# Gated experts: how many products run in three half-width passes, and which engine makes the weight parts

## What is computed

```python
# L0: 8 experts of width 176, two chosen of 8; shared width 352
w = jnp.zeros((n, E), x.dtype).at[jnp.arange(n)[:, None], idx].add(probs)
h = jax.nn.silu(jnp.einsum('tc,ech->eth', xf, W1)) * jnp.einsum('tc,ech->eth', xf, W2)
y = jnp.einsum('eth,ehc,te->tc', h, W3, w)
hs = jax.nn.silu(xf @ Ws1) * (xf @ Ws2)
y = y + (hs @ Ws3).reshape(b, t, c)
# L1: 16 experts of width 64, four chosen of 16 in two of four groups; shared width 128
h = jax.nn.silu(g) * u
yo = jnp.einsum('tei,ehi->teh', h, down_w)
routed = jnp.einsum('te,teh->th', combine, yo)
return (routed + shared).reshape(orig_shape)
```

## Time and profile before

| | us |
|---|---|
| median of three runs | 3198.48 |
| lowest and highest | 3195.55, 3201.10 |
| the profiled execution, whole | 3196.91 |
| its span, first to last instruction | 3195.1 |
| first stage, from the start of its first PE instruction to the end of its last add on DVE | 428.40 to 574.89 |
| second stage | 632.71 to 777.44 |
| third stage | 1322.74 to 1430.86 |
| fourth stage | 1472.89 to 1570.70 |

### The profile page before, as it was taken

One profiled execution on the slowest core, in us unless ns is written; L12 is line 12 of the kernel. 1 busy time (PEld: TensorE's weight loads), 2 busy tenths in 40 slices (PEclk: granted clock), 3 DMA queues, 4 the chain that ended last, 5 costly groups with the idle time before them and its releaser, 6 DMA issues. The chain is left out here.

```text
span 3195.1 us, 58999 instructions
## 1 busy us (share of the span) xinstructions
PE 2902.7 (91%) x22885; PEld 1670.8 (52%) x22885; DVE 2175.3 (68%) x4839; ACT 1643.5 (51%) x3325; POOL 1127.0 (35%) x536
## 2 busy tenths in 40 slices
PE   7898899998999999998968897888889899998998
PEld 3333344443899999543435454444453344574547
DVE  6777645556677777667588887877861559926991
ACT  3555453433333333436467766676753557725761
POOL 1111130002100000100088787877840209912980
PEclk8999999999555555799979999999999899999999
DMA  5344323022000000030532222222302001250224
GB/s 158 91 109 99 90 91 108 3 91 84 4 4 4 4 4 4 2 109 4 187 112 95 83 90 80 87 82 83 90 27 100 4 1 80 93 198 4 95 107 177
DMA packets 113495, 234.37 MB, mean 73 GB/s; under 512 B 13760, under 2 KB 50752, under 8 KB 104768
## 3 DMA queue, kind: packets, MB, share of 16 engines
q1 hardware_dynamic: 113216, 230.59, 22.5%
HBM read 185.71 MB, written 44.83 MB: 72 GB/s over the span
## 5 line engine op out<-in xcount | busy, mean ns | idle before, releaser
L2680 DVE TENSOR_TENSOR_SCAN s_hh<-psum,s_dbu 128x512 f32<-128x512 f32 x384 | 447.6, 1208 | 71.1 <-ACT psum L2292 70.2
L1404 PE MATMUL psum<-h_ring,h_parts 128*128 128x4 f16 x12264 | 477.9, 168 | 0.6 <-DVE h_ring L1547 0.5
L2550 POOL TENSOR_TENSOR s_dbu<-s_du,s_bb 128x1024 f32<-128x1024 f32 x191 | 446.4, 2359 | 67.1 <-DVE s_hh L2680 57.1
L1404 PEld LDWEIGHTS psum<-h_ring,h_parts 128*128 128x128 f16 x12264 | 429.7, 106 | 48.6 <-DVE h_ring L1547 0.9
L1466 ACT ACTIVATE h_now<-psum 128x16 f32<-128x16 f32 x1024 | 187.9, 184 | 324.4 <-PE psum L1404 318.2
L2292 ACT ACTIVATE psum<-s_delta,s_decay 128x512 f32<-128x512 f32 x384 | 256.6, 686 | 109.9 <-DVE s_hh L2680 107.8
L2184 PEld LDWEIGHTS psum<-w_c,s_term 128*128 128x128 f32 x1536 | 197.7, 149 | 136.3 <-issue 115.8
L1547 DVE TENSOR_SCALAR h_ring<-h_now 128x16 f16<-128x16 f32 x1024 | 178.8, 175 | 117.9 <-ACT h_now L1466 77.0
L990 POOL MEMSET r_weights<- 128x512 f32 x4 | 2.1, 524 | 720.4 <-POOLq L1356 510.9
L2184 PE MATMUL psum<-w_c,s_term 128*128 128x128 f32 x1536 | 229.7, 286 | 9.6 <-ACT s_y L2370 8.5
L1549 DVE SCALAR_TENSOR_TENSOR h_ring<-h_now,h_ring 128x16 f16<-128x16 f32 x1024 | 179.5, 175 | 35.2
(11 more groups left out here) (586 smaller groups left out, 6224.1 us busy)
## 6 DMA issues: line engine op xcount, KB each, us to landing
s_bb<-s_wide SPq DMA_DIRECT2D x192, 256.0 KB, 3.4
x_spill<-x_flip SPq DMA_DIRECT2D x28, 1024.0 KB, 3.9
f_share<-f_wide SPq DMA_DIRECT2D x208, 128.0 KB, 3.0
s_cc<-s_wide SPq DMA_DIRECT2D x60, 256.0 KB, 3.4
a_ks<-a_spread SPq DMA_DIRECT2D x96, 128.0 KB, 3.3
a_qs<-a_spread SPq DMA_DIRECT2D x96, 128.0 KB, 4.0
x_spare<-x_spill SPq DMA_DIRECT2D x4, 2048.0 KB, 7.6
x_raw<-x_spill SPq DMA_DIRECT2D x4, 2048.0 KB, 7.7
```

The costliest lines, as they stand in the source:

```text
L1404: mm = nc.tensor.matmul(here[:, cols], parts[:, part, GROUP * grp + p, :], ring[:, (i - 1) % RING, grp, cut, cols], start=False, stop=True ...
L2550: nc.gpsimd.tensor_tensor(dbu[:, s % D_RING], du[:, t % 2], both(bb[:, s % B_RING, :]), ALU.mult).then_inc(dbu_ready, 1)
L2680: nc.vector.tensor_tensor_scan(hh[:, s % 4, half, :], DECAYS[i % 3], dbu[:, s % D_RING, half, :], 0.0, ALU.mult, ALU.add).then_inc(scan_do ...
```

## The change

1. In the second, third and fourth stage the three passes begin with the first chunk (`CUT_FROM` 0). DVE cuts the first chunk's inputs itself, between the norm's first and second chunk (`cut_first_inputs`).
2. From the second chunk on, in all four stages, the down products listed in `twofold` are made in three passes too: the shared tiles and every second routed one, 8 of 14 and 5 of 9 in a chunk. ACT makes the high part of the hidden tile (`keep_hi`) and POOL the rest (`keep_lo`, an f32 and an f16 input in SBUF, f16 out), in a ring of six; weights' down parts are cut as well (`MATRICES` 3). Scales are fitted to that, and the add into the residual takes one.
3. In the third stage DVE makes the weights' parts: `make_cuts(0)` and `(1)` between the norm's chunks, `(2)` behind the router. The search for the largest weight is passed over PE within the norm (`behind`). In the first stage ACT and POOL make them as before, with the third matrix added.
4. `LAG` becomes 15 and 19 in the first and second stage, 27 in the third and fourth; `TURN_AT` 18 instead of 17 in the latter two; weighings from the second chunk on stand four iterations ahead of their down product instead of two (`SOON`).

```diff
...
-LAG, AHEAD, LOGITS_AT, SQUASH_AT, EXP_AT, TURN_AT, KEEP_AT = 15, 2, 1, 1, 5, 9, 9
+AHEAD, LOGITS_AT, SQUASH_AT, TURN_AT, KEEP_AT = 2, 1, 1, 9, 9
 TURN_MOST_AT, TOP_AT, SPREAD_MOST_AT, SCALE_AT, CUT_AT = 3, 1, 4, 2, (5, 6, 9)
-WEIGHTS_EARLY = False
-BESIDE = {2: (1,), 4: (2,), 5: (3, 4), 9: (5,)}
+LAGS, EXPS_AT, WEIGHTS_EARLY = (15, 19), (5, 6), False
+BESIDES = ({2: (1,), 4: (2,), 5: (3, 4), 9: (5,)}, {1: (1,), 2: (2,), 3: (3, 4), 5: (5,), 8: (6,)})
...
-LAG, AHEAD, LOGITS_AT, SQUASH_AT, EXP_AT, TURN_AT, KEEP_AT = 24, 2, 1, 1, None, 17, 17
-TURN_MOST_AT, TOP_AT, SPREAD_MOST_AT, SCALE_AT, CUT_AT = 2, 0, 3, 1, (3, 4, 6)
-WEIGHTS_EARLY = True
-BESIDE = {n: (k + 1,) for k, n in enumerate((3, 6, 8, 9, 10, 12, 13, 14, 15, 17, 18, 19, 20, 21, 22))}
+AHEAD, LOGITS_AT, SQUASH_AT, TURN_AT, KEEP_AT = 2, 1, 1, 18, 18
+LAGS, EXPS_AT, WEIGHTS_EARLY = (27, 27), (None, None), True
+BESIDES = 2 * ({n: (k + 1,) for k, n in enumerate((3, 6, 8, 9, 10, 12, 13, 14, 15, 17, 18, 19, 20, 21, 22))},)
...
+again = int(router.pack in g.cuts_made)
+g.cuts_made.add(router.pack)
+experts, LAG, BESIDE, EXP_AT = router.experts, router.LAGS[again], router.BESIDES[again], router.EXPS_AT[again]
+cuts_first, cuts_beside = not again and router.WEIGHTS_EARLY, not again and not router.WEIGHTS_EARLY
...
-CUT_FROM, SOON, PARTS_RING = EACH, 4, 6
+CUT_FROM, SOON, PARTS_RING = EACH if cuts_beside else 0, 4, 6
+twofold = [i for i in range(EACH, ALL) if i % EACH < SHARED or (i % EACH - SHARED) % 2]
+place_of = {i: n for n, i in enumerate(twofold)}
 COLS = w["down"].shape[1]
...
-most, inverse, raising, lowering, both_scale, out_scale = (scale[:, k:k + 1] for k in range(6))
+most, inverse, raising, lowering, both_scale, out_scale, full_scale = (scale[:, k:k + 1] for k in range(7))
...
-MATRICES = 2
-makes_cuts = router.pack not in g.cuts_made
-g.cuts_made.add(router.pack)
+MATRICES = 3
...
-        if i < 2:
+        if CUT_FROM == 0 and i == 0:
...
             if i % EACH == 0:
-                pe.wait_ge(x_cut, c)
-            if makes_cuts and i == CUT_FROM:
+                pe.wait_ge(x_cut, c + (CUT_FROM == 0))
+            if not again and i == CUT_FROM:
                 pe.wait_ge(lo_made, 1)
             three_products(bank[i % 2 * 2], 0, m, c).then_inc(gate_ready, 1)
-            pe.wait_ge(product_done, i - 1)
-            if makes_cuts and i == CUT_FROM:
+            if i >= 2:
+                pe.wait_ge(product_done, i - 1)
+            elif i == 0:
+                pe.wait_ge(norm.normed, 2)
+            if not again and i == CUT_FROM:
                 pe.wait_ge(lo_made, 2)
             three_products(bank[i % 2 * 2 + 1], 1, m, c).then_inc(up_ready, 1)
             return
...
+        if i in place_of:
+            if not again and i == twofold[0]:
+                pe.wait_ge(lo_made, 3)
+            pe.wait_ge(lo_kept, place_of[i] + 1)
+            slot = place_of[i] % PARTS_RING
+            nc.tensor.matmul(bank[4 + c % 2], cut_of(0, 2, m), h_parts[:, slot, 0, :], start=(k == 0), stop=False)
+            nc.tensor.matmul(bank[4 + c % 2], cut_of(1, 2, m), h_parts[:, slot, 0, :], start=False, stop=False)
+            nc.tensor.matmul(bank[4 + c % 2], cut_of(0, 2, m), h_parts[:, slot, 1, :],
+                             start=False, stop=(k == EACH - 1)).then_inc(down_done, 1)
+            return
...
-    norm.tensor(pe)
+    norm.tensor(pe, behind=(turn_most, spread_most) if cuts_first else ())
...
-        if makes_cuts and i == router.TURN_MOST_AT:
+        if cuts_beside and i == router.TURN_MOST_AT:
...
+    def keep_hi(j):
+        n = place_of[j]
+        if j % EACH < SHARED:
+            act.wait_ge(product_done, j + 1)
+        else:
+            act.wait_ge(weighed, routed_before(j) + 1)
+        if not again and n == 0:
+            act.wait_ge(lo_made, 3)
+        if n >= PARTS_RING:
+            act.wait_ge(down_done, twofold[n - PARTS_RING] + 1)
+        nc.scalar.copy(h_parts[:, n % PARTS_RING, 0, :], hid[:, j % RING, :]).then_inc(hi_kept, 1)
     norm.scalar(act)
-    for i in range(ALL):
+    for i in range(ALL + LAG - SOON + 1):
...
-        act.wait_ge(gate_ready, i + 1)
-        if i >= 2:
-            act.wait_ge(product_done, i - 1)
-        nc.scalar.activation(gate[:, i % 2, :], bank[i % 2 * 2], ACT.Silu,
-                             scale=inverse if i >= CUT_FROM else 1.0 / X_RAISED).then_inc(gated, 1)
-        if makes_cuts and i in router.CUT_AT[0:2]:
-            make_hi(router.CUT_AT.index(i))
+        if i < ALL:
+            act.wait_ge(gate_ready, i + 1)
+            if i >= 2:
+                act.wait_ge(product_done, i - 1)
+            nc.scalar.activation(gate[:, i % 2, :], bank[i % 2 * 2], ACT.Silu,
+                                 scale=inverse if i >= CUT_FROM else 1.0 / X_RAISED).then_inc(gated, 1)
+            if cuts_beside and i in router.CUT_AT:
+                make_hi(router.CUT_AT.index(i))
+        if i - LAG + SOON - 1 in place_of:
+            keep_hi(i - LAG + SOON - 1)
...
         pool.wait_ge(norm.normed, c + 1)
+        if CUT_FROM == 0 and c == 1:
+            pool.wait_ge(x_cut, 1)
         nc.gpsimd.tensor_copy(fixed(x_parts[:, 0, :], c), fixed(g.normed, c)).then_inc(x1_kept, 1)
-        pool.wait_ge(x1_kept, c)
+        pool.wait_ge(x1_kept, c + (CUT_FROM == 0))
         nc.gpsimd.tensor_tensor(fixed(x_parts[:, 1, :], c), fixed(g.normed, c), fixed(x_parts[:, 0, :], c), ALU.subtract).then_inc(x_cut, 1)
...
+    def keep_lo(j):
+        pool.wait_ge(hi_kept, place_of[j] + 1)
+        slot = place_of[j] % PARTS_RING
+        nc.gpsimd.tensor_tensor(h_parts[:, slot, 1, :], hid[:, j % RING, :], h_parts[:, slot, 0, :], ALU.subtract).then_inc(lo_kept, 1)
...
+    if cuts_beside:
         make_lo(0)
         make_lo(1)
     cut_inputs(2)
+    if cuts_beside:
+        make_lo(2)
     cut_inputs(3)
+    for j in twofold:
+        keep_lo(j)
...
-                                       scalar=inverse if i >= CUT_FROM else 1.0 / X_RAISED,
+                                       scalar=1.0 / X_RAISED if i < CUT_FROM else both_scale if i in place_of else full_scale,
                                        in1=gate[:, i % 2, :], op0=ALU.mult, op1=ALU.mult).then_inc(product_done, 1)
...
+        if cuts_beside and i == router.TOP_AT:
+            keep_top()
+        if cuts_beside and i == router.SCALE_AT:
...
-        nc.vector.tensor_scalar(raising, lowering, W_RAISED, None, ALU.mult).then_inc(scales_ready, 1)
+        nc.vector.tensor_scalar(both_scale, lowering, H_RAISED / (W_RAISED * X_RAISED), None, ALU.mult)
+        nc.vector.tensor_scalar(out_scale, most, most, most, ALU.mult, ALU.mult).then_inc(scaled, 1)
+        nc.vector.tensor_scalar(raising, lowering, W_RAISED, None, ALU.mult)
+        nc.vector.tensor_scalar(full_scale, lowering, lowering, H_RAISED / X_RAISED, ALU.mult, ALU.mult)
+        dve.wait_ge(scaled, 3)
+        nc.vector.tensor_scalar(out_scale, out_scale, 1.0 / (W_RAISED * H_RAISED), None, ALU.mult).then_inc(scales_ready, 1)
...
         dve.wait_ge(down_done, (c + 1) * EACH)
-        nc.vector.tensor_tensor(fixed(g.resid, c), fixed(g.resid, c), bank[4 + c % 2], ALU.add).then_inc(resid_done, 1)
+        if c * EACH >= CUT_FROM:
+            nc.vector.scalar_tensor_tensor(out=fixed(g.resid, c), in0=bank[4 + c % 2], scalar=out_scale, in1=fixed(g.resid, c),
+                                           op0=ALU.mult, op1=ALU.add).then_inc(resid_done, 1)
+        else:
+            nc.vector.tensor_tensor(fixed(g.resid, c), fixed(g.resid, c), bank[4 + c % 2], ALU.add).then_inc(resid_done, 1)
...
+    def make_cuts(matrix):
+        here = slice(matrix * COLS, (matrix + 1) * COLS)
+        kind = ("gate", "up", "down")[matrix]
+        if matrix == 0:
+            dve.wait_ge(scales_ready, 1)
+        nc.vector.tensor_scalar(cut[:, 0, here], w[kind], raising, None, ALU.mult).then_inc(hi_made, 1)
+        dve.wait_ge(hi_made, matrix + 1)
+        nc.vector.scalar_tensor_tensor(out=cut[:, 1, here], in0=w[kind], scalar=raising, in1=cut[:, 0, here],
+                                       op0=ALU.mult, op1=ALU.subtract).then_inc(lo_made, 1)
+    def cut_first_inputs():
+        dve.wait_ge(norm.normed, 1)
+        nc.vector.tensor_copy(fixed(x_parts[:, 0, :], 0), fixed(g.normed, 0)).then_inc(x1_kept, 1)
+        dve.wait_ge(x1_kept, 1)
+        nc.vector.tensor_tensor(fixed(x_parts[:, 1, :], 0), fixed(g.normed, 0), fixed(x_parts[:, 0, :], 0),
+                                ALU.subtract).then_inc(x_cut, 1)
+    if cuts_first:
         for matrix in range(MATRICES):
             find_most(matrix)
         keep_most()
-    for c in range(CHUNKS):
-        norm.vector(dve, c)
-    if makes_cuts and not router.WEIGHTS_EARLY:
+        keep_top()
+    norm.vector(dve, 0)
+    if CUT_FROM == 0:
+        cut_first_inputs()
+    if cuts_first:
+        make_scales()
+    norm.vector(dve, 1)
+    if cuts_first:
+        make_cuts(0)
+    norm.vector(dve, 2)
+    if cuts_first:
+        make_cuts(1)
```

(11 more changed lines are left out.)

36 lines of the change are left out of this document (18 added, 18 removed).

## The result

The changed kernel takes 3201.32 us (median of 20 runs, 3197.83 to 3207.16), the kernel before 3196.05 us on the same chip (20 runs, 3192.71 to 3201.10): ratio 1.0017, 95% interval 1.0010 to 1.0023. It is slower by 5.3 us; I had forecast 0.7 us less. The profiled execution has a span of 3198.0 us, 2.9 more than before.

A forecast was written before the change was run, and what follows sets the result against it. PE was taken to bound each stage up to its last product, DVE and POOL together the changed drains. Stages of +0.6, -4.2, +0.7 and +2.2 summed to -0.7 us: 3197.8 us from the median 3198.5, range 3174 to 3213.

The forecast's parts named there:

- Two inputs in SBUF beside a reading POOL: All stages: DVE's weighing with two SBUF inputs and POOL's `keep_lo` exclude each other, lengthening drains by 2.3 to 7.1 us.
- how long POOL holds DVE: Drains: whole instruction assumed; a first-stage row suggested 0.85 of 1.16 us, making the sum 5.5 us lower.
- The drain term: After gate and up, DVE and POOL together set the pace: drains of 16.2, 19.7, 28.9 and 28.9 us.
- The third stage's start: Fourth chunk normed 5.4 us later, but DVE's 4.91 us wait gone; transposition 2.5 us earlier (-4 to +1).
- the router's 24.9 us: Third stage: time from the router's start to the transposition, taken as in the fourth stage.
- the third search: Third stage: a third search for a largest weight, 1.3 us, falls into a gap before the norm's first operation.
- rival 3: The change does less than it says, for instance weight parts hold the third stage up: +4, 3202 us; chance 0.06.
- The middle: Beside gate and up PE stays the bound, 4.09 us per two iterations, so the full gain is taken there.
- G: End of gate and up in each stage, predicted to move by -1.7, -9.95, -6.4 and -4.9 us.
- Rival 1: Drains run at PE's pace, 12.0, 15.0, 21.0 and 21.0 us: together -26 us, 3172 us; chance 0.13.
- Rival 2: PE's clock falls to 1.2 GHz in the drains: +21 us for half of them, 3219 us; chance 0.15.
- The row of the seventh layer: Profile row cited for a clock fall in the drains: granted clock 0.84 with PE busy 2.97 of 5 us.

The follow-up runs named there:

- the last kernel above: A few three-pass downs put back into all four drains, all three matrices cut again, against the kernel described before it: ratio 0.9967 to the unchanged kernel, median 3186.8 us.
- the kernel described before it: Changed kernel with three-pass downs only beside gate and up, third stage's norm first, less work ahead of its router: ratio 0.9954 to the unchanged kernel, median 3179.71 us.

## Why the prediction was wrong, point by point

**Two inputs in SBUF beside a reading POOL** was right and carried the forecast: all four drains became longer, by 2.5, 5.4, 8.2 and 8.2 us, where I had 2.3, 5.8, 7.1 and 7.1, and the run without POOL's reads brings them to PE's own pace (12.0, 15.0, 21.1, 21.1; I had 12.0, 15.0, 21.0, 21.0). The question of how long POOL holds DVE is answered too: where the two engines alternate in the drain above, a pair takes 1.56 us. My sum had 0.98 + 0.61 = 1.59 for it, and the row in the first stage, with 0.85 in place of 0.98, would have made it 1.46 (over 44 operations that is 5.7 us, where I wrote 5.5). It was misleading. Nor do the two exclude each other to the last: their own lengths, 0.68 and 1.16, add up to 1.84. One instruction of each, shortest, median and longest in ns, in the fourth stage's drain after:

```profile
L1097 DVE TENSOR_TENSOR f_hid<-f_hid,f_share x17: 678/1245/1640, 1548.0 to 1567.8; 128x512 f32<-128x512 f32 x17
L1033 POOL TENSOR_TENSOR f_left<-f_hid,f_left x11: 1154/1597/1602, 1547.6 to 1567.3; 128x512 f16<-128x512 f32 x11
```

**The drain term was 1.0 us too small in the last two stages.** For nine products my figures give 8 x 0.61 + 5 x 0.98 = 9.78 us, and 9.88 were measured, so the steady pace accounts for 0.3 of it. My sum had no place for the adds, three to a drain, which stand in DVE's queue between the weighings (1547.37, 0.66 us to the next operation), with POOL working beside them for all but 0.2. That these make up the rest fits but was not tried by itself. In each of the two stages the drain is 1.0 us of the forecast's miss.

**The third stage's start was the step that failed.** I had the router start 21.8 us into the stage and the transposition at +46.7 in place of +49.2, on the ground that DVE's wait of 4.91 us was gone. The norm and weight parts came as fast as I had them and faster (fourth norm at +14.9; I had +16.8). But I had written down PE standing idle there and charged nothing for it. The clock fell to 1.2 GHz in its waits, the logits cost 6.84 instead of 3.64 us, and the router began at +23.2; the transposition came at +49.5, 2.8 us after my +46.7. Filling the waits with idle products moved the router's first step to +19.3 and the transposition to +45.4. So the idle time that I priced at nothing cost 4.1 us.

Two smaller terms of the same sum were wrong, and partly cancelled. I took the router's 24.9 us over from the fourth stage; here it takes 26.3, and 26.1 with the waits filled, so 1.2 us of it is not the clock's, and what it is stays open. And I put the third search at nothing, though it delays the norm by 1.4 us in the kernels with the norm first. The start was late enough in my sum for that all the same: I had the fourth norm at +16.8.

My rival 3 named the mechanism, scores after products at the lower clock, and its sign, a transposition later than +49, is what was measured (+49.5). Its price of +4 and its 3202 us are near too, but there is luck in that: it had the fourth norm at 1342, +19.3, where it came at +14.9, and drains of the forecast's length. I gave it a chance of 0.06.

**The middle** was right: beside gate and up a three-pass down gains its 0.215 us (6 us for 28 of them, in the kernel with those alone). G moved by -2.0, -10.7, -3.6 and -4.7; I had -1.7, -9.95, -6.4, -4.9, so three of four within 0.8.

**Rival 1** (drains at PE's pace) did not happen in the change, but is what happens once the shared reading is gone: its 3172 us against spans of 3176.1 and 3175.3. **Rival 2** (the clock falls in the drains) is wrong: 1.00 with PE busy 18.68 of 25 us. The row of the seventh layer was no guide.

**The size of the whole.** The stages' marks explain 3.5 us of a profiled difference of 2.9, and the medians differ by 5.3. The other 2.4 us lie between executions, not in a place that I can name: the same instructions at the start of a stage took up to 3 to 4 us more or less from one kernel to the next, with the clock at the logits, and the rest of the kernel, untouched by any of the runs, varies by 10. One such place is in the first layer. These are the same 6.8 us of the changed kernel and of the kernel with the filled waits, whose first stage begins at 428.55 and 425.17 us:

```profile
388.70:395.50 6.80, 6.66 (x23) 2.07 (x15) 3.06 (x14) 2.12 (x5) 0.64 (x1) 0.50 0.01 2
```

```profile
388.70:395.50 6.80, 5.50 (x30) 1.99 (x29) 5.12 (x23) 4.16 (x9) 1.20 (x2) 1.00 0.00 0
```

The forecast's own bound of 6.4 us for "no change" is wider than the difference measured; its direction, 0.7 us down, was wrong. With both misses of the drains and the third stage's 2.8 us put right it would have been +4.1 us.

## What to carry to other kernels

Before work is moved to GpSimd, list what VectorE does at the same time with two inputs in SBUF, and add the two engines' times for each stretch: where another engine is busy for longer (here the middle, under gate and up), the sum is hidden, and where none is (the drain), it is the time. A change that is good in one stretch and bad in another should be made only in the first; that alone turned 1.0017 into 0.9967, intervals well apart. And a wait that is put in front of TensorE is to be charged not only with its length but also with what the products behind it cost at the lower clock.

## What the runs showed of the hardware

- VectorE's two-input operation in SBUF and GpSimd's reading operation shut each other out nearly wholly and in turn: 0.68 and 1.16 us become 1.64 and 1.60 when they alternate, waiting included, and a pair takes 1.56. With one of VectorE's inputs in PSUM, or with GpSimd only writing, both keep their own durations.
- A scaling of VectorE with a single SBUF tensor and f16 output meets GpSimd too, and the one that began first kept its time. The first scaling below began 0.15 us ahead of a cast of GpSimd and took 0.81 us, as it does alone; the cast took 1.13 instead of 0.61. The second one (1329.69, shown above) began while GpSimd's two-input operation was still running, and took 1.11. The Trainium skill has this as well, in the same section: `tensor_scalar` can enter a two-port mode and then contends. The trace agrees.

```profile
1326.68 0.81 DVE L1118 TENSOR_SCALAR cut_l1f<-w_l1f,scale_l1f 128x1152 f16<-128x1152 f32 x1
```

```profile
1326.83 1.13 POOL L1012 CAST f_xparts<-normed 128x512 f16<-128x512 f32 x1 [7.66 <-DVE normed L141]
1328.04 2.15 POOL L1014 TENSOR_TENSOR f_xparts<-normed,f_xparts 128x512 f16<-128x512 f32 x1
```

- TensorE's granted clock stayed at 1.00 through 25 us of waits of about a microsecond each (busy 18.68 us), and fell to 0.50 after waits of 1.49 and 2.51 us with three passes between them. It also fell where nothing had made TensorE wait for more than 0.22 us since the stage's first product: in the second stage of the last kernel above the logits took 4.66 us, and the stretch with them and the one behind show 0.63 and 0.68, while the kernel described before it has 1.00 there and 3.63 us. These are the two kernels' stretches with the logits:

```profile
637.60:642.60 5.00, 5.00 (x36) 3.64 (x36) 2.76 (x19) 2.58 (x5) 2.40 (x3) 1.00 0.00 0
```

```profile
638.70:643.70 5.00, 5.00 (x28) 4.02 (x28) 1.80 (x17) 1.53 (x4) 2.35 (x3) 0.63 0.00 0
```

Between these two the second stage's transposition moved by 3.2 us. What decides it stays open.
